# Two image ends and the last strip of an attention and convolution kernel: steps moved to VectorE, a projection in halves, a strip buffer of its own

## What is computed

```python
def _L0_conv_ref(x, ac_w, ac_b, qkv_w, proj_w, proj_b):
    g = (x * ac_w[None, :, None, None] + ac_b[None, :, None, None]) * x
    g = jnp.clip(g, 0.0, 6.0)
    qkv = jnp.einsum('bchw,dc->bdhw', g, qkv_w)
    ...
    attn = jnp.einsum('wnqd,wnkd->wnqk', q, k) * scale      # windows of 8 x 8 pixels, 16 heads of 8
    attn = jax.nn.softmax(attn, axis=-1)
    o = jnp.einsum('wnqk,wnkd->wnqd', attn, v)
    ...
    out = jnp.einsum('bchw,dc->bdhw', o, proj_w) + proj_b[None, :, None, None]

x = x + _L0_conv_ref(_gn(x), ...)       # attention in windows, added to the image
x = x + _L1_conv_ref(_gn(x), W, bias)   # 3 x 3 convolution of the normed image, added to it
```

## Time and profile before

| | |
|---|---|
| median of 3 runs | 1161.74 us |
| the three runs | 1161.74, 1167.04, 1161.53 us |
| the profiled execution | 1167.43 us, of which the profile's span is 1165.7 us |
| busy PE, DVE | 1010.4 us (87%), 974.0 us (84%) |
| busy ACT, POOL | 785.3 us (67%), 499.3 us (43%) |
| seam of the first, of the second image | 486 to 502 us, 1012 to 1028 us |
| convolution stage of the first, of the second image | 502 to 636 us, 1028 to 1163 us |

### The profile page before, as it was taken

The page is one execution under the profiler, slowest core; times in us unless marked ns, Lnnn a source line. Parts: engine busy times, 40 slices in busy tenths (PEclk is TensorE's granted clock), DMA queues, the critical chain, the costliest instruction groups (busy, mean ns, idle before and its releaser), DMA issues.

```text
span 1165.7 us, 52675 instructions
## 1 busy us (share of the span) xinstructions
PE 1010.4 (87%) x23011; PEld 583.5 (50%) x23011; DVE 974.0 (84%) x1310; ACT 785.3 (67%) x1326; POOL 499.3 (43%) x467
## 2 busy tenths in 40 slices
PE   0279888998998989779999999999999999679996
PEld 0145555555655556434444565665655555334442
DVE  6787778887887879689999888898988876379997
ACT  0247777877877768556565787888888777555663
POOL 5314444454454435403335454454545453403335
PEclk9979999999999989889999999999999999889999
DMA  8355555544555435402435554544454444001112
GB/s 316 115 152 152 150 139 172 146 133 133 169 162 159 124 87 155 122 1 95 140 111 197 166 151 135 152 140 138 130 159 128 129 141 115 4 1 55 73 66 98
DMA packets 117221, 148.98 MB, mean 128 GB/s; under 512 B 25344, under 2 KB 91264, under 8 KB 115968
## 3 DMA queue, kind: packets, MB, share of 16 engines
q1 hardware_dynamic: 116992, 145.62, 41.2%
HBM read 76.35 MB, written 67.11 MB: 123 GB/s over the span
## 4 chain that ended last, share of the span: by engine, by line
PE 50%; DVE 18%; DMA 12%; issue 9%; SPq 7%; ACT 3%; POOL 1%; POOLq 0%; DVEq 0%; ACTq 0%
PE ps L1002 9%; PE ps L983 8%; DMA q_bd<-stack_scratch 7%; PE ps L1010 6%; PE ps L969 6%; PE ps L1087 5%; DVE work L858 5%; PE ps L937 4%; PE ps L938 4%; PE ps L939 4%; DVE work L854 4%; SPq L306 3%; DMA stack_scratch<-qk 3%; PE ps L956 2%; SPq L290 2%
## 5 line engine op out<-in xcount | busy, mean ns | idle before, releaser
L755 DVE TENSOR_REDUCE m_all<-ps 128x16 f32<-128x1024 f32 x256 | 313.3, 1224 | 110.5 <-PE ps L969 109.0
L476 ACT ACTIVATE work<-ps,ws 128x1024 f32<-128x1024 f32 x256 | 284.5, 1111 | 66.1 <-PE ps L983 62.3
L405 POOL TENSOR_SCALAR work<-work 128x256 f32<-128x256 f32 x128 | 108.8, 850 | 414.7 <-DVE work L743 354.3
L969 PEld LDWEIGHTS ps<-k_pl,q_bd 48*64 48x64 f16 x8192 | 90.2, 110 | 173.6 <-issue 111.7
L1002 PE MATMUL ps<-work,v_ext 128*32 128x64 f32 x8192 | 173.1, 225 | 4.4 <-issue 4.4
L983 PE MATMUL ps<-q_bd,k_pl 128*64 128x256 f16 x2048 | 165.5, 284 | 7.5 <-ACT work L476 3.2
L969 PE MATMUL ps<-k_pl,q_bd 48*64 48x64 f16 x8192 | 118.8, 197 | 55.2 <-issue 32.5
L937 PE MATMUL ps<-work,c_hi 128*128 128x512 f16 x384 | 147.8, 385 | 13.9 <-DVE work L858 13.9
L1002 PEld LDWEIGHTS ps<-work,v_ext 128*32 128x32 f32 x8192 | 129.9, 111 | 45.9 <-issue 41.3
L938 PE MATMUL ps<-work,c_lo 128*128 128x512 f16 x384 | 147.5, 384 | 0.0
L939 PE MATMUL ps<-work,c_hi 128*128 128x512 f16 x384 | 147.2, 383 | 0.0
(11 more groups left out here) (122 smaller groups left out, 1600.0 us busy)
## 6 DMA issues: line engine op xcount, KB each, us to landing
stack_scratch<-qk SPq DMA_DIRECT2D x128, 256.0 KB, 2.4
q_bd<-stack_scratch SPq DMA_DIRECT2D x256, 96.0 KB
k_pl<-stack_scratch SPq DMA_DIRECT2D x128, 192.0 KB, 3.7
stack_scratch<-qk SPq DMA_DIRECT2D x128, 128.0 KB, 2.6
out_dram<-img SPq DMA_DIRECT2D x32, 512.0 KB, 2.9
img<-in_x_dram SPq DMA_DIRECT2D x8, 1024.0 KB, 14.5
work<-in_x_dram SPq DMA_DIRECT2D x16, 512.0 KB, 5.2
img<-in_x_dram SPq DMA_DIRECT2D x16, 512.0 KB, 4.3
```

Of the source, the lines that this page charges most:

```text
L405: g.tensor_scalar(near[h], near[h], -2.0, None, ALU.add).then_inc(less_done, 1)
L476: a.activation(probs[h][:, p % 2, :], ps[:, ST_B:ST_B + 2, :].rearrange("p w t -> p (w t)"), ACT.Exp, scale=ws[:, R_EXP:R_EXP + 1]).then_i ...
L755: v.tensor_reduce(m_all[:, 0, :, p], ps[:, S_B:S_B + 2, :].rearrange("p r (a k) -> p (r a) k", k=WIN), AX.X, ALU.max).then_inc(max_done, 1)
L969: mm = t_.matmul(ps[64 * w:64 * w + 64, S_B + r, at:at + WIN], q_bd[rows, md, r, g, j, tok], k_pl[rows, md, g, tok], start=True, stop=True)
```

## The change

1. The last unit of each image (unit 31) ends by other steps. Half 1 of its quotient is done by DVE (`last_quotient`) right behind `scale`, in place of POOL; POOL only counts up the semaphores. PE projects it in two matmuls of 256 columns each, the first of which waits only for half 0, and writes the pixels in the image's order at once. While that goes on, ACT adds the bias to the 512 pixels of the image (in place of scaling the projection), and DVE adds the scaled projection from PSUM to them by one instruction (`last_residual`) in place of ACT and POOL, behind the statistics of units 29 and 30.
2. In the first strip of each image PE takes all matmuls of a plane that need `x_hi` alone (six) ahead of the three that need `x_lo`.
3. The last strip of the second image has a buffer of its own (in `v_ext`, which is free by then), so that ACT's `bases` waits for no addition; DVE adds it to the image in place of POOL, by two instructions, and SP waits for these.

```diff
--- before.py
+++ after.py
@@ -121,6 +121,12 @@
         x_hi, x_lo = x_both[:, 0, :, :, :], x_both[:, 1, :, :, :]
         c_out = [part(6912 + i * 1024, 1024).rearrange("p (r c) -> p r c", r=CROWS) for i in range(OUTS)]

+        c_last = v_ext[:, :, :, :, :, :].rearrange("p b n k s y -> p (b n k s y)")[:, 0:1024].rearrange("p (r c) -> p r c", r=CROWS)
+
+        def result(n):
+
+            return c_last if n == BATCH * CUNITS - 1 else c_out[n % OUTS]
+
         raw_qkv = part(0, 384).rearrange("p (t c) -> p t c", t=3)
         raw_proj = part(384, 128)
         raw_conv = part(2048, C * TAPS).rearrange("p (i k) -> p i k", k=TAPS)
@@ -154,14 +160,14 @@
         m_in = sem("m_in", 64)
         st_done = sem("st_done", 4); exp_done = sem("exp_done", 4); pv_done = sem("pv_done", 4)
         ln_done = sem("ln_done", 2); guess_done = sem("guess_done", 2)
-        quot_out = sem("quot_out", 2); less_done = sem("less_done", 2); o_done = sem("o_done", 2)
+        quot_out = sem("quot_out", 2); less_done = sem("less_done", 2); o_done = sem("o_done", 2); last_o_done = sem("last_o_done")
         proj_done = sem("proj_done"); res_done = sem("res_done"); x1_done = sem("x1_done")
         bn_done = sem("bn_done")

         cx_done = sem("cx_done"); planes_done = sem("planes_done", PLANES)
         x_hi_done = sem("x_hi_done", PLANES); x_lo_done = sem("x_lo_done", PLANES); carried = sem("carried")
         conv_done = sem("conv_done", PLANES); base_out = sem("base_out", 2); ends_out = sem("ends_out"); sums_out = sem("sums_out")
-        cadd_done = sem("cadd_done", 2)
+        cadd_done = sem("cadd_done", 2); last_added = sem("last_added", 2)
         out_done = [sem(f"out_done{e}", 16) for e in range(2)]; next_in = sem("next_in", 16); side_in = [sem(f"side_in{e}", 16) for e in range(2)]; side_done = sem("side_done", 2)

         w_in = sem("w_in"); x_in = [sem(f"x_in{i}") for i in range(LOADS)]
@@ -351,7 +357,10 @@
                 def conv_one(t, top, bottom):
                     n = t + b * CUNITS
                     more = b + 1 < BATCH
-                    after(sp, cadd_done, n)
+                    if n == BATCH * CUNITS - 1:
+                        after(sp, last_added, 0)
+                    else:
+                        after(sp, cadd_done, n)
                     after(sp, out_done[n % 2], n // 2 - 1)
                     sp.dma_start(out[b, :, t * CROWS:t * CROWS + CROWS, :], img[:, t * CROWS:t * CROWS + CROWS, :]).then_inc(out_done[n % 2], 16)
                     if more and t:
@@ -413,11 +422,16 @@

                 def one(i, m, live):
                     n = i + b * UNITS
-                    if live(-2):
+                    if live(-2) and i - 2 != UNITS - 1:
                         quotient(n - 2, 1)
+                    elif live(-2):
+                        pool.sem_inc(less_done, 1)
                     if live(3) and n + 3 != SEAM_G - 1:
                         weak_part(n + 3)
-                    if live(-3):
+                    if live(-3) and i - 3 == UNITS - 1:
+                        after(pool, proj_done, n - 3)
+                        pool.sem_inc(o_done, 1)
+                    elif live(-3):
                         row, col = pixels(i - 3)
                         here = img[:, bass.ds(row, WS), bass.ds(col, UCOL)]
                         after(pool, res_done, n - 3)
@@ -441,7 +455,8 @@
                 def conv_one(t, top, bottom):
                     if top and b + 1 < BATCH:
                         weak_part(SEAM_G - 1)
-                    residual(t, t + b * CUNITS)
+                    if b + 1 < BATCH or not bottom:
+                        residual(t, t + b * CUNITS)
                 conv_units(conv_one)

         @block.scalar
@@ -523,7 +538,12 @@
                         exps(n - 1, 3)
                     if live(4):
                         strong_part(n + 4)
-                    if live(-2):
+                    if live(-2) and i - 2 == UNITS - 1:
+                        row, col = pixels(UNITS - 1)
+                        here = img[:, row:row + WS, col:col + UCOL]
+                        after(act, gpre_done, n - 2)
+                        a.activation(here, here, ACT.Identity, bias=vecs[:, 2:3]).then_inc(res_done, 1)
+                    elif live(-2):
                         after(act, proj_done, n - 2)
                         after(act, x1_done, n - 3)
                         a.activation(res.rearrange("p (y n x) -> p n y x", y=WS, n=UW),
@@ -557,9 +577,10 @@
                 def bases(n):

                     after(act, conv_done, n, 2)
-                    after(act, cadd_done, n - OUTS)
+                    if n < BATCH * CUNITS - 1:
+                        after(act, cadd_done, n - OUTS)
                     for e, (col, bias) in enumerate(((R_CONV, vecs[:, 3:4]), (R_MINUS, cf[:, C_MINUS:C_MINUS + 1]))):
-                        a.activation(outputs(c_out[n % OUTS], e), ps[:, PLANES * (n % 2) + 1, :], ACT.Identity,
+                        a.activation(outputs(result(n), e), ps[:, PLANES * (n % 2) + 1, :], ACT.Identity,
                                      scale=ws[:, col:col + 1], bias=bias).then_inc(base_out, 1)

                 def conv_one(t, top, bottom):
@@ -743,6 +764,22 @@
                     v.tensor_tensor(quot[h].rearrange("p (s t) -> p s t", s=2), ps[:, PV_B + h, :].rearrange("p (s t) -> p s t", s=2),
                                     guess[h].unsqueeze(1).broadcast_to([P, 2, HALF]), ALU.mult).then_inc(quot_out, 1)

+                def last_quotient(d):
+
+                    after(dve, proj_done, d - 1)
+                    after(dve, quot_out, d)
+                    link(v.tensor_scalar(near[1], near[1], -2.0, None, ALU.add))
+                    v.tensor_tensor(o_n[:, HALF:2 * HALF], near[1], scaled[1], ALU.mult).then_inc(last_o_done, 1)
+
+                def last_residual(d):
+
+                    row, col = pixels(UNITS - 1)
+                    here = img[:, row:row + WS, col:col + UCOL]
+                    after(dve, res_done, d)
+                    after(dve, proj_done, d)
+                    v.scalar_tensor_tensor(out=here, in0=ps[:, GB, :].rearrange("p (y c) -> p y c", y=WS),
+                                           scalar=ws[:, R_RES:R_RES + 1], in1=here, op0=ALU.mult, op1=ALU.add).then_inc(x1_done, 1)
+
                 def side_half(k):

                     after(dve, side_in[(k // 2) % 2], k // 4)
@@ -766,6 +803,8 @@
                         row_max(n + 1, 2)
                     if live(-1):
                         scale(n - 1, 1)
+                        if i - 1 == UNITS - 1:
+                            last_quotient(n - 1)
                     if n == SIDE_T:
                         spread(1, SIDE_SC, SIDE_NORM)
                     if live(1):
@@ -786,6 +825,8 @@
                     if live(2):
                         row_max(n + 2, 0)
                     if live(-3):
+                        if i - 3 == UNITS - 1:
+                            last_residual(n - 3)
                         row, col = pixels(i - 3)
                         after(dve, x1_done, n - 3)
                         v.bn_stats(st[:, i - 3, :],
@@ -825,14 +866,14 @@
                     bank = PLANES * (n % 2)
                     after(dve, base_out, n)
                     after(dve, conv_done, n)
-                    c = halves(c_out[n % OUTS])
+                    c = halves(result(n))
                     v.scalar_tensor_tensor(out=c, in0=ps[:, bank:bank + PLANES:PLANES - 1, :], scalar=ws[:, R_CONV:R_CONV + 1], in1=c,
                                            op0=ALU.mult, op1=ALU.add).then_inc(ends_out, 1)

                 def middle_sums(n):

                     after(dve, ends_out, n)
-                    c = halves(c_out[n % OUTS])
+                    c = halves(result(n))
                     v.scalar_tensor_tensor(out=c, in0=ps[:, PLANES * (n % 2) + 2, :].unsqueeze(1).broadcast_to([P, 2, 512]),
                                            scalar=ws[:, R_CONV:R_CONV + 1], in1=c, op0=ALU.mult, op1=ALU.add).then_inc(sums_out, 1)

@@ -893,6 +934,12 @@
                         low(3, t + 1, n + 1)
                     if bottom:
                         sums(n)
+                        if not more:
+                            after(dve, sums_out, n)
+                            c = result(n).rearrange("p r (c e) -> p r c e", e=2)
+                            x1 = img[:, t * CROWS:t * CROWS + CROWS, :].rearrange("p r (c e) -> p r c e", e=2)
+                            for e, op in enumerate((ALU.add, ALU.subtract)):
+                                v.tensor_tensor(x1[:, :, :, e], x1[:, :, :, e], c[:, :, :, e], op).then_inc(last_added, 1)
                     if more and t == 8:
                         sloped(SEAM_G)
                         multiplied(SEAM_G)
@@ -1083,8 +1130,18 @@
                             after(pe, k_lo_done, n + 3)
                         else:
```

(27 more changed lines are left out.)

## The result

| | before | changed |
|---|---|---|
| median of 20 runs each | 1165.72 us | 1160.20 us |
| lowest and highest | 1155.76 to 1176.10 | 1149.24 to 1165.92 |
| mean, standard deviation | 1165.4, 5.3 | 1159.0, 5.1 |
| the profiled execution, its span | 1167.43, 1165.7 | 1162.85, 1161.1 |

The ratio is 0.9948, with a 95% interval of 0.9925 to 0.9971: 6.0 us less, between 3.4 and 8.7. Against 1165.72 the changed kernel is 0.5% faster. The time itself, 1160.20, lies above the forecast range (1149.5 to 1157.5). The three runs of before that stood ahead had a median of 1161.74, and twenty of it have 1165.72: 4 us of the miss were in the starting point. In all that follows a run more than 1.5% above the fastest of its kernel is left out of medians, means and ratios; the traced run of `before_again` (1181.66 us) is such a one.

A forecast was written before the change was run, and what follows sets the result against it. VectorE, without a gap, bounds the two convolution stages; at the seams the engines run in single file. 2 × 3.3 + 2 × 0.8 + 1.5 = 9.7 us off 1161.74 gives 1152.0 us, range 1149.5 to 1157.5.

The forecast's parts named there:

- Gain 3.3 us a seam: Between unit loop and convolution stage, once per image: the shorter chain saves 3.3 us, bounds 2.0 and 3.7.
- the rival of a replaced wait: At both seams GpSimd's addition blocks VectorE's quotient, or the first half projection isn't ahead: 1.3 us less each; chance 0.12.
- TensorE's clock should not matter here: At the seam, VectorE's two statistics end at 489.05, later than the half projection at either clock (488.4 or 488.9).
- one of the forecast's own signs of being wrong: At the seam: the forecast is wrong if the projection's end, and not VectorE, starts the SCALAR_TENSOR_TENSOR.
- 0.8 us a seam should go through: First strip of each convolution stage: matmuls start 0.8 us earlier and all of it arrives; bounds 0 and 1.0.
- early matmuls are for nothing: Rival at the first strip: VectorE is bound by its own work from the start, giving 1153.6 us; chance 0.08.
- Gain 1.5 us: Kernel's end: own buffer and VectorE additions for the last strip save 1.5 us, bounds 0.9 and 1.8.
- The floor that the transfers set: Kernel's end: two transfers of 1.25 us from 1160.5 end at 1163.2, limiting the engines' 1.76 us gain to 1.5.
- I carry the gain over to the median: 1161.74 − 9.7: Whole kernel: all terms lie outside the unit loop, so 9.7 us comes off the three-run median, giving 1152.0.
- a rival about the *changed* kernel's median: Spread of runs: the changed kernel's median falls 5.3 us higher, at 1157.3, within 0.5% of 1161.74; chance 0.12.
- The slower rival: Second image's unit loop: its earlier start brings more clock falls, 2.4 us each; seven give 1169 us; chance 0.03.
- the 0.1 that I had named as a sign: Second image's unit loop: the forecast is wrong if units differ from 11.83 us each by more than 0.1.

The follow-up runs named there:

- `before_again`: The kernel before, unchanged, run and traced again against itself: 1171.37 us, ratio 0.9986.
- `top_only`: The kernel before with only the first strip's new order of matmuls (x_hi first): 1171.41 us, ratio 1.0003 against before.
- the first comparison: The whole change against the kernel before, 20 runs each: 1160.20 against 1165.72 us, ratio 0.9948.
- the other two differ by 8.3 and 11.6: The whole change timed twice more against the kernel before: 1166.86 us, ratio 0.9937, and 1164.09 us, ratio 0.9919.
- `warm_no_top`: Changed kernel plus unread matmuls in both seams and unit 29's statistics ahead of the last scaling, first strip in old order: 1159.76 us, 0.9883 against before.

## Why the prediction was right or wrong

- **"Gain 3.3 us a seam": right.** Measured 3.39 and 3.31. The quotient was ready 0.85 after the scaling's end (0.78 forecast: 0.29 for the 0.30, 0.42 for the 0.38, waits of 0.10 and 0.04), the two statistics took 1.28 (1.3), the new step 0.73 and 0.75 (0.70). GpSimd's L438 ended 0.30 before VectorE's first quotient step, so the rival of a replaced wait did not come. ScalarE's bias cost nothing, as put.
- **"TensorE's clock should not matter here": wrong, by a little.** A half projection was put at 0.53 or 1.03; it took 0.70 at the full clock and 1.18 almost wholly at the half, and another 0.12 lie between its end and the next step, which the sum did not have. In four of the six seams of the three traces of the changed kernel VectorE still came last; in the other two the projection's end started the SCALAR_TENSOR_TENSOR, one of the forecast's own signs of being wrong, for 0.07 and 0.27 us.
- **"0.8 us a seam should go through": wrong, about half of it did.** TensorE did start 0.8 earlier (8.09 instead of 8.89 after the statistics). The step that failed is that the whole earlier start was passed on to the strips behind, as if TensorE did the same work in each of these microseconds; it worked at half speed until its clock rose. I had named the case in which the clock rises no earlier, and gave it 0, and one in which it rises in proportion, 1.0. The runs show neither: with the rise where it was, the start counts half, 0.4. The rest is where the rise fell. In the second stage it came 0.1 later, which leaves 0.37. In the first it came 1.0 earlier, worth 0.5, and the 0.3 of strip 13 went off again, which leaves 0.57: nearer to 0.8 by luck. The rival "early matmuls are for nothing" is refuted by the table of F, though in the first image of `top_only` it would have looked true (C 141.28 against 141.30).
- **"Gain 1.5 us" at the end: 1.77.** The additions met GpSimd's and took 1.65, 0.36 more than a pair of such steps alone (1.29), as forecast (0.4). The Trainium skill, "SBUF — State Buffer", section "Who interferes with whom", says that VectorE steps with two SBUF inputs and GpSimd's SBUF reads exclude each other for a whole instruction. The 1.65 here and the 1.37 in strip 13 agree: in both the VectorE step ends some 0.55 us after GpSimd's. The floor that the transfers set was put 0.25 too high. Counted from the second sum of strip 30 they were to begin at 5.3 and end at 8.0 us; the slices above have them from 5.17 to 7.76.
- **The sum: 9.4 in the profile, 9.7 forecast.** The too large 0.8 (0.7 us over both seams) was made up in part by the end and the seams, so the near hit of the sum is in part luck.
- **"I carry the gain over to the median: 1161.74 − 9.7": this is the step that failed.** The term that was mis-sized is the 1161.74, the time the gain was taken from. The three runs' median was 1161.74; twenty runs of the same kernel had 1165.72, a deviation of 5.3 and a width of 20. The forecast from 1165.72 would have been 1156.0, inside the range given. I had seen that two of four known times lay 5.5 us higher, and put a chance of 0.12 on it as a rival about the *changed* kernel's median, instead of asking how far the median of three can be off: at a deviation of 5.3 that is some 3.5 us either way. That leaves 4.2 us, from 1156.0 to 1160.2. In the first comparison the means differ by 6.4 and not 9.5, two standard errors of 1.6; the other two differ by 8.3 and 11.6. Taken together, 8.4, they are within the error of the 9.5. Whether the 4.2 is chance alone, or the change also costs a microsecond or two in the loops, stays open.
- **The slower rival** (falls of the clock in the loops): the falls are real. Late in the second image's loop the changed trace has one: a group of 16 matmuls that takes 1.05 at the full clock took 1.70.

```profile
1004.68 1.07 PE L1030 MATMUL ps<-q_bd,k_pl 128*64 128x256 f16 x8 [0.62 <-ACT work L491]
...
1006.53 1.70 PE L1057 MATMUL ps<-work,adds 128*32 128x256 f32 x16
```

  The 2.83 that D was longer are 0.09 a unit over its 30 or so units, under the 0.1 that I had named as a sign; and D is as long with the old seam as with the new one, so this trace does not point to the change.

## What to carry to other kernels

Before a gain of under 1% is carried over to a measured time, ask how far that time itself is known: here the loops that nobody touched moved by more than the whole gain from one execution to the next, and only segments cut at the changed places showed it (9.5 us; the new seam within 0.3 and the end within 0.1 from trace to trace). A chain that passes through four engines for one small tile is worth moving to the engine that must come last anyway, but then count what is already queued on it: here the two statistics set the new length, and the half projection did where TensorE ran most of it at its half clock. And where TensorE starts a stage at the half clock, work given to it earlier counts half until the clock rises.

## What the hardware showed that I had not expected

- The length of a stage bound by TensorE at its start followed 126.0 to 126.2 us + (start + clock's rise)/2 over thirteen traces (second image), while the rise itself came between 2.8 and 5.6 us after the first matmul (11.0 to 13.9 after the statistics) in kernels whose loops and seams had no added matmuls.
- Ten matmuls of 512 columns that end 0.3 to 1.1 us before the stage brought the full clock by 8.12 to 8.82 us after the statistics in three seams, and in one, of `warm_no_top`, not before 12.02.
- The same 10635 matmuls of a unit loop took between 377.6 and 387.7 us, and with TensorE almost never idle the runs still spread with a deviation of 3 to 4 us.
